# Stage 1 of a fused transformer layer: where the key norm's small steps and the query scales run, and when two loads are asked for

## The reference, cut to what matters

```python
q = einsum('bsd,ed->bse', x, Wq)          # 32 heads of 128
k = einsum('bsd,ed->bse', x, Wk)          # 8 heads of 128
v = einsum('bsd,ed->bse', x, Wv)
q = rope(rmsnorm(q, q_norm_w), pos)       # rmsnorm: t * rsqrt(mean(t*t) + 1e-6) * w
k = rope(rmsnorm(k, k_norm_w), pos)
...                                       # scores against cached pages and own keys, softmax, values, Wo
```

## Time and profile before

| | us |
|---|---|
| median of three runs | 3061.29 |
| profiled execution, its own time | 3071.46 |
| its span | 3069.9 |
| PE busy in it | 3027.6 (99%) |
| key blocks, from the start of project 1 to that of turn(15) | 452.0 to 575.9 |
| stage 2's first matmul | 617.1 |

### The profile page before, as it was taken

How to read it: one execution, slowest core, us unless ns; L and a number is a source line. 1 busy time by engine, 2 the same in 40 slices (tenths; PEclk the granted TensorE clock), 3 DMA queues, 4 the chain that set the end, 5 groups by cost and what they waited for, 6 DMA issues and landing times.

```text
span 3069.9 us, 91713 instructions
## 1 busy us (share of the span) xinstructions
PE 3027.6 (99%) x36256; PEld 2351.8 (77%) x36256; DVE 1860.2 (61%) x3587; ACT 1543.4 (50%) x2949; POOL 595.0 (19%) x1430
## 2 busy tenths in 40 slices
PE   8999998999999999999999999999999999999999
PEld 7777777767777777777777888888888888888887
DVE  6777768477888877888886444442333333544445
ACT  6666655377777777777776222221333333322221
POOL 0000001055455455455452000000000000200000
PEclk9999999999999999999999999999999999999999
DMA  5333334566676676676677344412333333743311
GB/s 167 97 110 105 115 110 131 166 208 205 211 220 204 206 219 206 210 220 205 209 219 229 110 126 125 124 65 100 104 103 104 97 110 100 240 148 110 109 41 55
DMA packets 508661, 456.02 MB, mean 149 GB/s; under 512 B 33985, under 2 KB 470593, under 8 KB 503746
## 3 DMA queue, kind: packets, MB, share of 16 engines
q1 hardware_dynamic: 475010, 362.80, 39.3%
q0 software_dynamic: 33344, 88.46, 8.9%
HBM read 321.03 MB, written 130.02 MB: 147 GB/s over the span
## 4 chain that ended last, share of the span: by engine, by line
PE 78%; DMA 1%; issue 0%; DVE 0%; ACT 0%; DVEq 0%; SPq 0%
PE ps_o L1009 18%; PE ps_scores L993 16%; PE s_ps L58 8%; PE s_ps L60 8%; PE s_ps L59 8%; PE s_ps_proj L58 5%; PE s_ps_proj L59 5%; PE s_ps_proj L60 5%; PE s_ps_o L1542 1%; PE s_ps_scores L1518 1%; PE yv_ps L60 1%; PE yv_ps L59 1%; PE yv_ps L58 1%; PE s_ps L1717 0%; PE s_ps L1708 0%
## 5 line engine op out<-in xcount | busy, mean ns | idle before, releaser
L1009 PEld LDWEIGHTS ps_o<-weights_t,v_all 32*128 32x128 f32 x17408 | 514.0, 187 | 111.1 <-issue 110.3
L1009 PE MATMUL ps_o<-weights_t,v_all 32*128 32x128 f32 x17408 | 564.4, 277 | 5.6 <-issue 3.7
L993 PE MATMUL ps_scores<-k_slot,q_slot 128*32 128x288 f32 (+1 forms) x8192 | 525.9, 397 | 7.0 <-PEq L98 4.8
L898 ACT ACTIVATE probs<-masked,shift 128x544 f32<-128x544 f32 x512 | 382.9, 748 | 248.1 <-DVE shift L944 246.6
L944 DVE CUSTOM_DVE_ANT_0 masked<-ps_scores,reach,scale_now 128x544 f32<-128x544 f32 x512 | 390.2, 762 | 179.2 <-PE ps_scores L993 175.0
L993 PEld LDWEIGHTS ps_scores<-k_slot,q_slot 128*32 128x32 f32 x8192 | 241.2, 110 | 201.6 <-issue 9.6
L957 DVE STREAM_TRANSPOSE weights_t<-probs 128x544 f32<-128x544 f32 x512 | 376.8, 736 | 23.5 <-ACT probs L903 10.3
L903 ACT ACTIVATE probs<-probs,inv 128x544 f32<-128x544 f32 x512 | 375.7, 734 | 0.0
L1101 ACT ACTIVATE s_h_hi<-s_h_raw 128x2048 fp32r<-128x2048 f32 x64 | 122.8, 1919 | 488.2 <-PE s_ps L60 472.3
L84 POOL COPY k_slot<-k_pool 128x256 f32 x1024 | 359.3, 410 | 34.8 <-DMA k_pool<-kpool_in 19.1
L58 PE MATMUL s_ps_proj<-y_hi,s_w_hi 128*128 128x512 f32 x640 | 253.1, 395 | 0.0
(11 more groups left out here) (201 smaller groups left out, 4723.0 us busy)
## 6 DMA issues: line engine op xcount, KB each, us to landing
v_all<-vpool_in SPq DMA_DIRECT2D x1024, 128.0 KB, 3.0
qT_scratch<-k_pool SPq DMA_DIRECT2D x32, 1024.0 KB, 5.1
q_slot<-qT_scratch POOLq DMA_DIRECT2D x64, 512.0 KB, 3.5
oT_scratch<-o_t POOLq DMA_DIRECT2D x128, 256.0 KB, 5.1
s_h_raw<-oT_scratch SPq DMA_DIRECT2D x32, 1024.0 KB, 5.8
aT_scratch<-s_o_t SPq DMA_DIRECT2D x32, 1024.0 KB, 5.7
s_h_raw<-aT_scratch SPq DMA_DIRECT2D x32, 1024.0 KB
w_raw<-w_in SPq DMA_DIRECT2D x11, 1024.0 KB, 8.0
```

Of the source, the lines that this page charges most:

```text
L898: act.activation(probs[:, k % BUF, :], masked[:, k % 2, :], ACT.Exp, bias=shift[:, k % BUF:k % BUF + 1], scale=-1.0, accum_out=total[:, k ...
L993: m = pe.matmul(ps_scores[q * S:(q + 1) * S, k % 2, cols], q_slots[j][:, head, r * S:(r + 1) * S], k_slots[j][:, pages, head * PSIZE:(head ...
L1009: m = pe.matmul(ps_o[:, q, 0:GS], v_all[rows, j, t, e * D:(e + 1) * D], weights_t[rows, g, :, t * S:(t + 1) * S], start=t == 0, stop=t == NPP)
```

## The change

Four things are changed.

1. Of `norm`'s six small steps DVE keeps the reciprocal; the other five go to POOL, with a semaphore between the two (`root_inverted`) and one that counts POOL's steps (`norm_step`). Two sets of `nw` alternate.
2. DVE makes the reciprocal a unit ahead: in unit r, after by_sin, it does `invert(r + 1)`, which waits for the root of unit r + 1. `invert(0)` stands ahead of unit 0, and ACT makes root 0 straight behind squares 0.
3. The q root (ACT), `q_norm` (DVE) and the scale copies (POOL) come after the key blocks. Their scratch is now by_cos and by_sin.
4. SP asks for the weights of block 11 in unit 5 of the first key block, doesn't wait for the q scales any more, and loads one pool piece in each unit of the second key block, not two in each of four.

```diff
         @block.sync    (k_block)
-                next_w(9 + cb)
                 if cb == 0:
+                    next_w(9)
...
-                else:
-                    sp.wait_ge(q_scale_done, SEQ * G)
...
                     if cb == 0:
                         for k in range(2):
                             load_pool(u // 4 * 3, u % 4 * 2 + k, POOL_PIECES)
-                    elif 1 <= u <= 4:
-                        for k in range(2):
-                            load_pool(1, 2 * u - 2 + k, POOL_PIECES)
+                        if u == 5:
+                            next_w(10)
+                    else:
+                        load_pool(1, u, POOL_PIECES)

         @block.gpsimd    (the 16 scale copies move behind the load_q and load_k_own)
+            for r in range(RU):
+                cb, u = r // UN, r % UN
+                now = nw[:, r % 2, :, :]
+                ss = sums[:, HK + cb, u * 8:(u + 1) * 8]
+                pool.wait_ge(root_done, r + 1)
+                if r >= 2:
+                    pool.wait_ge(rotated, r)
+                pool.tensor_scalar(now[:, 0, :], ss, 1.0 / D, EPS, ALU.mult, ALU.add).then_inc(norm_step, 1)
+                pool.wait_ge(root_inverted, r + 1)
+                pool.tensor_tensor(now[:, 2, :], now[:, 1, :], now[:, 1, :], ALU.mult).then_inc(norm_step, 1)
...                                        (three more steps, each behind a wait on norm_step)

         @block.scalar
-                    if r == 0:
-                        act.wait_ge(q_rotated, QM + 2)
-                        act.activation(q_root, q_sums, ACT.Sqrt, ...).then_inc(q_root_done, 1)
...
             for u in range(2):
                 squares_of(u, HK, u)
-            for u in range(2):
                 root_of(0, u)
...
                 v_copy(VU + RU + u, u, VU + RU // 2 + u // 2 * 2)
+                if u == 1:
+                    act.wait_ge(rotated, RU + 1)
+                    act.activation(q_root, q_sums, ACT.Sqrt, ...).then_inc(q_root_done, 1)

         @block.vector
+            def invert(r):
+                dve.wait_ge(root_done, r + 1)
+                dve.reciprocal(nw[:, r % 2, 1, :], root[:, r, :]).then_inc(root_inverted, 1)
...                                        (in rotate, behind by_sin)
-                if norms:
-                    norm(*norms)
+                if norms and r + 1 < RU:
+                    invert(r + 1)
...                                        (ahead of the product with the norm)
+                    dve.wait_ge(norm_step, (r + 1) * 5)
...
+            invert(0)
             for cb in range(2):
                 for u in range(UN):
                     rotate(cb * UN + u, u, tab_k, (cb, u))
                     if 1 <= u <= KC:
                         split(10 + cb, cb, u - 1)
-                    if cb == 0 and 2 <= u:
-                        q_norm(u - 2)
+            for k in range(UN - 2):
+                q_norm(k)
```

More of the change, by code:

```diff
@@ L119, in stage1 @@
         root = hold(nc.sbuf_tensor("root", [P, 2 * UN, 8], F32))
-        nw = hold(nc.sbuf_tensor("nw", [P, 4, 8], F32))
+        nw = hold(nc.sbuf_tensor("nw", [P, 2, 4, 8], F32))
         eps = hold(nc.sbuf_tensor("eps", [P, 1], F32))
@@ L141, in stage1 @@
         dve_step = hold(nc.semaphore("dve_step"))
+        norm_step = hold(nc.semaphore("norm_step"))
+        root_inverted = hold(nc.semaphore("root_inverted"))
         halves_done = hold(nc.semaphore("halves_done"))
@@ L188, in stage1 @@
         q_sums = sums[:, 0:HK, :].rearrange("p h n -> p (h n)")
[L189 to L192, removed]
+        q_root, q_mean = by_cos[:, 0:NQ], by_cos[:, NQ:2 * NQ]
+        q_inv, q_step = by_sin[:, 0:NQ], by_sin[:, NQ:2 * NQ]
         @block.sync
@@ L320, in _ @@
                                          sums_rows.rearrange("p (b s) -> p b s", s=S)[:, :, 0]).then_inc(q_sums_kept, 1)
[L322 to L327, removed]
+            for r in range(RU):
[8 more added lines that the diff above has]
+                pool.tensor_tensor(now[:, 2, :], now[:, 1, :], now[:, 1, :], ALU.mult).then_inc(norm_step, 1)
+                pool.wait_ge(norm_step, r * 5 + 2)
+                pool.tensor_tensor(now[:, 2, :], now[:, 2, :], now[:, 0, :], ALU.mult).then_inc(norm_step, 1)
+                pool.wait_ge(norm_step, r * 5 + 3)
+                pool.tensor_scalar(now[:, 2, :], now[:, 2, :], -0.5, 1.5, ALU.mult, ALU.add).then_inc(norm_step, 1)
+                pool.wait_ge(norm_step, r * 5 + 4)
+                pool.tensor_tensor(now[:, 3, :], now[:, 2, :], now[:, 1, :], ALU.mult).then_inc(norm_step, 1)
             pool.wait_ge(turn_done, RU + 2)
@@ L335, in _ @@
             c["load_q"](pool, 1, 1)
+            pool.wait_ge(q_inv_done, 1)
+            inv4 = q_inv.rearrange("p (e h b) -> p h e b", e=2, h=SEQ)
+            scale4 = c["q_scale"][:, :, :].rearrange("p b (e g) -> p g e b", g=G)
+            for g in range(G):
+                for q in range(SEQ):
+                    pool.tensor_copy(scale4[q * S:(q + 1) * S, g, :, :], inv4[g * S:(g + 1) * S, q, :, :]).then_inc(q_scale_done, 1)
+            pool.wait_ge(q_scale_done, SEQ * G)
             pool.wait_ge(c["pool_loaded"], 16 * 4 * POOL_PIECES)
@@ L432, in k_block @@
                         split(cb, 10 + cb, u)
-                    if r == 0:
-                        act.wait_ge(q_rotated, QM + 2)
-                        act.activation(q_root, q_sums, ACT.Sqrt, bias=eps[:, 0:1], scale=1.0 / D).then_inc(q_root_done, 1)
             x_high_piece(0)
@@ L467, in _ @@
                 v_copy(VU + RU + u, u, VU + RU // 2 + u // 2 * 2)
+                if u == 1:
+                    act.wait_ge(rotated, RU + 1)
+                    act.activation(q_root, q_sums, ACT.Sqrt, bias=eps[:, 0:1], scale=1.0 / D).then_inc(q_root_done, 1)
         @block.vector
@@ L599, in rotate @@
                     dve.wait_ge(halves_done, norms[0] * UN + u + 1)
+                    dve.wait_ge(norm_step, (r + 1) * 5)
                     m = dve.tensor_tensor(turning[:, u % 2, :].rearrange("p (h d) -> p h d", d=D),
                                           turning[:, u % 2, :].rearrange("p (h d) -> p h d", d=D),
-                                          nw[:, 3, :].rearrange("p (h o) -> p h o", o=1).to_broadcast([P, 8, D]), ALU.mult)
+                                          nw[:, u % 2, 3, :].rearrange("p (h o) -> p h o", o=1).to_broadcast([P, 8, D]), ALU.mult)
                 m.then_inc(rotated, 1)
```

## The result

Twenty runs of each: 3056.56 us median after (3050.64 to 3060.43), 3061.43 before (3058.68 to 3067.47). The ratio of times is 0.9979, 95% interval 0.9972 to 0.9985, which is 4.6 to 8.6 us faster. The medians themselves are 4.9 us apart. The forecast was 3055.4 us, 5.9 us faster.

What follows compares the result with a forecast made beforehand. PE, 99% busy, was taken to bound the kernel, with DVE as full; -7.8 (chain) + 1.4 (GpSimd contention) + 0.5 (late store) = -5.9 us, from 3061.29 to 3055.4 us. Range for 8 in 10 runs: 3050.5 to 3063.

Steps and rivals of the forecast that it cites:

- The chain over two units: Key blocks: projection, root r+1, early reciprocal and by_sin close a loop, 13.60 us per pair, 14.02 with split; -7.8 us.
- What VectorE waits: Sign in the key blocks: DVE's reciprocal waits for ACT's root some 15 times, 0.8 to 2.5 us each, about 21.
- GpSimd beside VectorE: Key blocks: POOL's small steps cost DVE 0.2 us, once per pair, +1.4 us (0 to 12); low bound 0.
- my high bound: Key blocks: 4 POOL steps of 0.43 us ahead of DVE's operations, 1.7 us a unit.
- The late store: Unit 15: a pool piece behind the last key store delays the second v copy, +0.5 us (0 to 1.0).
- the new place of root 0: First unit: root 0 straight behind squares 0 puts invert(0) at 454.9 and by_cos(0) at 455.2; called hidden.
- My walk: Key blocks, followed from squares 0: projection 3 at 465.65, projection 17 at 562.5, turn(15) at 568.1 instead of 575.87.
- The clock in the new stalls: Rival: clock falls to 1.2 GHz after the chain's PE stalls, up to 2.0 us each; +8.1, 3069.4 us; 6%.
- POOL first: Rival: POOL's four steps get ahead of DVE's sum, product and split each time; +4.6 us, 3065.9 us; 9%.
- Nothing gained: Rival: contention of about 0.7 a unit, one clock fall and the late store eat most; 3060 us; 15%.
- The free pace: Rival: DVE finds each root ready and PE sets the pace in the key blocks; -15.6 us, 3046.2 us; 5%.
- The signs: Expected in the profile, among them: no PE wait over 2 us before 575, clock at 2.4 GHz throughout.

Runs made afterwards that it cites:

- The moved reciprocal (both places): Changed kernel with the reciprocal for unit r+1 behind the product, or between sum and product: ratio to before 0.9951 and 0.9936, turn(15) 107.47 and 107.51 us.
- the additional steps: Changed kernel with four more small GpSimd products (128x8) in each unit, behind its first product: one run, 3060.12 us, turn(15) at 115.43 us.
- root order: Kernel before with root 0 straight behind squares 0 on ScalarE, not behind squares 1: ratio to before 0.9982 (0.9973 to 0.9991).
- the better version: Changed kernel, reciprocal behind product, VectorE's weight splits a unit later, first v copy ahead of turn 15's, stage 2's first q and k load later: 3043.10 us.
- norm on DVE: Changed kernel with all six small norm steps back on VectorE in their own unit: ratio to before 0.9951 (0.9937 to 0.9964), turn(15) at 107.18 us.
- weights early: Kernel before with only the last weights asked for in unit 5 of the first key block: ratio to before 0.9987 (0.9978 to 0.9996).
- scales behind: Kernel before with only the query scales made behind the key blocks: ratio to before 0.9989 (0.9980 to 0.9998).

## Why the prediction was right, point by point

- **The chain over two units.** Forecast 13.60 and 14.02 us a pair, measured 13.51 and 13.88. Turn(15) was forecast at 568.1 and started at 567.08. The links that I took too long are above all reciprocal to sum (0.23, measured 0.12) and sum to product (1.26, measured 1.23). The moved reciprocal (both places) shows that this chain, and no other, set the pace.
- **What VectorE waits.** Forecast about 21 us in 0.8 to 2.5, measured 26.2 in 16 waits of 0.6 to 2.8. The count includes the first wait ahead of unit 0.
- **GpSimd beside VectorE.** Forecast +1.4 us, measured about 0: the term was mis-sized, and the low bound was right. POOL's two long steps wait for DVE's, 0.85 to 1 us each, and have the time. The Trainium skill's rule in "SBUF — State Buffer", that the two exclude each other, agrees with POOL's 1.05 and 1.18 us rows: in all 15 units in which they meet, DVE's operation had begun before these two. POOL's first step begins 0.07 us ahead of the sum (473.77 and 473.84), and the sum is not longer for it (1.20 us). With the additional steps POOL came first at the product, and that cost DVE 0.03 us and not the 0.43 a step of my high bound.
- **The late store.** Forecast +0.5, measured none: the second v copy started 7.58 us behind turn(15), 7.82 before. In its place came something that I had not priced there: the half clock behind the wait of 2.16 us, some 8 matmuls with 0.2 us each lost; turn(15) to stage 2 takes 42.45 us for 41.25, 1.2 more. I had used that very wait's row before as evidence that waits of this length leave the clock alone. One row was too little for it.
- **The sum.** In the trace it is -8.7 + 0 + 0 + 1.2 = -7.5 us by the start of stage 2, where I had -7.8 + 1.4 + 0.5 = -5.9. The chain is most of it and was right; that the total lies so near to the measured 4.6 to 8.6 is in part luck, for the two prices that weren't there stand against a longer gain and a fall that I hadn't priced. The 0.5 was worked out from sizes, and no run shows it.
- **The free part that wasn't.** I called the new place of root 0 hidden, at cost 0. It is worth 5.9 us at the unit where it stands. My walk had it in, since it started from root 0 at 454.9, so the sum was right and the attribution wrong: a walk gives the end, it doesn't say which edit brought it.
- **The four parts.** At turn(15), alone against before: weights 5.2, scales 5.1, root order 4.4. The norm's move costs 8.0 against the same kernel without it. 16.7 gained, 8.0 given back, 8.7 left.
- **The rivals.** The clock in the new stalls: no fall behind any of the eight, of 0.5 to 1.2 us. POOL first: its four steps behind the reciprocal did not come first in the changed kernel, and where the additional steps made it so it cost 0.3 us in all. Nothing gained, within 3 us of before: the interval of 4.6 to 8.6 us excludes it. The free pace: it was there to be had, one operation further on.
- **The signs.** Two of them failed as they were written: there is a PE wait over 2 us before 575, at 570.27, since the old wait ahead of the second half of v comes sooner with everything else; and the clock was not at 2.4 GHz throughout. The others held, some by a little over their sizes: ACT has no wait for weights at the seam, and the gather is done at 597.7, before the last v copy at 604.9.

## What to carry to other kernels

Work that is taken ahead on an in-order engine brings its wait ahead too: ask not how early the result is wanted, but what stands behind the wait in the queue, and whether that releases the very work that is waited for. If it does, a loop closes, and the pace is its length over the units that it spans; shorten it below the bounding engine's need and all of the loss goes at once. A lighter engine is no gain where its work was hidden (whether DVE's small steps would cost anything in the better version, with its later splits, was not run), and in a change of several parts each part needs its own run.

## What the runs showed of the hardware that I had not expected

- A wait of PE of 2.15 us at the same place was followed by half clock (1.2 GHz) in two of the traces (the changed kernel and "root order") and by full clock in seven (before, norm on DVE, both moves of the reciprocal, weights early, scales behind, more POOL steps). Why is not settled.
- The same wait of 3.0 us was followed by a projection of 7.15 us in one kernel and of 8.36 in another. A stretch at half clock has no fixed price.
- A GpSimd operation of 128x8 takes 0.20 us, the same as VectorE's reciprocal of that size, and 1.05 to 1.19 us when it begins just behind a VectorE sum or product of 128x1024 with two SBUF inputs. Where GpSimd's began first (more POOL steps), VectorE's product took 1.26 us for 1.23.
